# A decoder of two layers on one core: the latent mask added by VectorE, contexts in one run, two stage borders and the experts' order rearranged

## What is computed

```python
# latent attention: queries from the 64 latents (the layer's x), keys and values
# from 64 context tokens and the 64 latents
kv = concat([layer_norm(ctx, g1, b1), ln_lat]) @ Wkv        # 128 tokens per batch
weight = q @ k.T * scale                                   # 16 heads, 64 x 128
weight = where([mask, ones(64)], weight, -max)             # mask only on the 64 context tokens
out = softmax(weight) @ v @ Wout
x = layernorm(x + out)
# experts
gate, idx = max(softmax(x @ router)), argmax(...)
expert e: relu(rows @ w1[e] + b1[e]) @ w2[e] + b2[e]       # its first 512 tokens
x = layernorm(x + gate * expert_output)
```

## Time and profile before

| | |
|---|---|
| three runs | 1677.36, 1677.72, 1684.27 us (median 1677.72) |
| the profiled execution | 1676.6 us, its span 1674.9 us, granted clock 0.989 |
| block 1, block 2, block 3 | to about 390, to about 1044, to the end |
| one pair in the middle of block 3 | 16.20 us |
| busy share of the span | TensorE 96%, weight loads 80%, VectorE 71%, ScalarE 54%, GpSimd 40% |
| DMA | 82.3 MB, 49 GB/s on average |

### The profile page before, as it was taken

The page is one execution under the profiler, slowest core; times in us unless marked ns, Lnnn a source line. Parts: engine busy times, 40 slices in busy tenths (PEclk is TensorE's granted clock), DMA queues, the critical chain, the costliest instruction groups (busy, mean ns, idle before and its releaser), DMA issues. The chain is left out here.

```text
span 1674.9 us, 52009 instructions
## 1 busy us (share of the span) xinstructions
PE 1605.6 (96%) x18188; PEld 1336.8 (80%) x18188; DVE 1183.3 (71%) x3386; ACT 908.5 (54%) x2619; POOL 677.0 (40%) x1070
## 2 busy tenths in 40 slices
PE   7999999998999999999999998899999999999795
PEld 6887788787777777777777776899999999999563
DVE  6889888676777776767777775467777777777654
ACT  5777777643455444544554444565655655656241
POOL 3666666312333333333333332234434444344345
PEclk9999999999999999999999999999999999999998
DMA  3214221121220001110000010121221212212331
GB/s 103 66 47 121 69 56 55 43 64 45 51 53 26 25 27 30 29 28 25 25 25 25 25 31 23 37 60 48 56 60 43 61 41 61 55 47 59 92 98 30
DMA packets 157654, 82.30 MB, mean 49 GB/s; under 512 B 17641, under 2 KB 153115, under 8 KB 157568
## 3 DMA queue, kind: packets, MB, share of 16 engines
q1 hardware_dynamic: 154800, 77.68, 17.4%
q0 software_dynamic: 2048, 3.15, 0.6%
q10 hardware_dynamic: 720, 0.33, 0.1%
HBM read 61.03 MB, written 21.27 MB: 49 GB/s over the span
## 5 line engine op out<-in xcount | busy, mean ns | idle before, releaser
L1477 PE MATMUL bank<-diff_xT,diff_w_score 128*128 128x128 f32 x2048 | 257.0, 279 | 0.7 <-ACT diff_xT L1594 0.7
L1477 PEld LDWEIGHTS bank<-diff_xT,diff_w_score 128*128 128x128 f32 x2048 | 239.3, 192 | 22.6 <-issue 20.2
L1601 ACT ACTIVATE diff_keys<-bank 128x512 f32<-128x512 f32 x256 | 152.4, 595 | 162.2 <-PE bank L1477 162.2
L2273 POOL TENSOR_TENSOR lat_prob<-lat_prob,lat_inv_sum 128x512 f32<-128x512 f32 x128 | 133.4, 1042 | 208.7 <-DVE lat_inv_sum L2198 207.8
L1792 POOL TENSOR_TENSOR diff_prob<-diff_prob,diff_inv_sum 128x512 f32<-128x512 f32 x64 | 67.1, 1049 | 369.6 <-DVE diff_inv_sum L1694 369.6
L2073 ACT ACTIVATE lat_prob<-bank,lat_neg_max 128x128 f32<-128x128 f32 x512 | 180.5, 372 | 1.0 <-DVE lat_neg_max L2218 1.0
L2084 ACT ACTIVATE lat_query<-bank 128x512 f32<-128x512 f32 x128 | 76.5, 597 | 174.3 <-PE bank L1967 159.2
L1997 PE MATMUL bank<-lat_catT,lat_query 128*128 128x128 f32 x1024 | 142.4, 282 | 3.9 <-ACT lat_query L2084 3.9
L1967 PE MATMUL bank<-lat_catT,lat_w_score 128*128 128x128 f32 x1024 | 139.5, 280 | 2.2 <-ACT lat_catT L2065 1.0
L1997 PEld LDWEIGHTS bank<-lat_catT,lat_query 128*128 128x128 f32 x1024 | 125.2, 193 | 15.8 <-issue 10.6
L1977 PE MATMUL bank<-lat_probT,lat_c_rep 32*128 32x256 f32 x2048 | 128.3, 387 | 3.1 <-DVE lat_z L2203 3.1
(11 more groups left out here) (274 smaller groups left out, 3674.4 us busy)
## 6 DMA issues: line engine op xcount, KB each, us to landing
lat_c_rep<-cat SPq DMA_DIRECT2D x128, 128.0 KB
stage<-low_y SPq DMA_DIRECT2D x64, 64.0 KB, 1.6
diff_x_rep<-stage SPq DMA_DIRECT2D x128, 32.0 KB, 1.7
lat_c_t<-cat SPq DMA_DIRECT2D x32, 128.0 KB, 2.2
exp_w<-in_L_ffn_w_dram SPq DMA_DIRECT2D x16, 256.0 KB
expert_rows<-latw_zeros SPq DMA_DIRECT2D x4, 548.0 KB, 5.4
exp_rows<-expert_rows SPq DMA_DIRECT2D x8, 274.0 KB
low_x_t<-in_x_dram SPq DMA_DIRECT2D x32, 64.0 KB, 1.9
```

The lines of the kernel that those rows point to most:

```text
L1477: last = nc.tensor.matmul(ring[(k + d) % 2][:, j * P:(j + 1) * P], w_score[:, H1 * (k // 2) + HS * d + 4 * (k % 2) + j, :], xT[:, :], star ...
L1601: nc.scalar.activation(keys[:, k // 2, 4 * (k % 2):4 * (k % 2) + 4, :].rearrange("p h t -> p (h t)"), ring[(k + d) % 2][:, :], ACT.Copy).t ...
L2273: nc.gpsimd.tensor_tensor(prob[:, q, :, :], prob[:, q, :, :], inv_sum[:, q, :, None].to_broadcast([P, 4, T]), ALU.mult)\
```

## The change

- **Mask.** The identity matmul L2000 goes. VectorE adds the mask in place in PSUM (128 x 256 elements, bf16 mask) before it takes the maximum, and waits on its own semaphore `masked` between the two.
- **Contexts.** Both halves of `contexts(i-1)` stand in c=3, one behind the other. `outputs(i-2)` is cut into 5, 6 and 5 matmuls for c = 0, 1, 2. `z`, its statistics and the variance move from c=1 to c=2 on VectorE, the power from c=2 to c=3 on GpSimd.
- **First border.** TensorE's last feed-forward products stand ahead of the barrier, with five matmuls without use behind them; ScalarE takes the last of the scaled weight copies from VectorE.
- **Second border.** VectorE's three copies of `w_vo` and SyncE's last store of `lat` stand behind the barrier, in block 3; twelve matmuls without use instead of eight. TensorE waits for the `w_vo` copies before the first scores, not before the stage.
- **Last scatter of rows.** GpSimd leaves out `dump` and prepares the token's number before it waits for the destination.
- **Experts.** Three banks for the output products; the rows of e+1 are transposed before the hidden products of e; the hidden products of 7 come before the outputs of 6.
- **Semaphores** of block 3 are no longer cleared by a `give_back` of their own.

```diff
@@ FeedForward.tensor, and its block @@
-        if drain:
-            self.drain(pe, slot)
-        else:
-            pe.wait_ge(self.low.qT_ready, NI)
-            self.slots(pe, slot, between)
+        pe.wait_ge(self.low.qT_ready, NI)
+        self.slots(pe, slot, between)
+        self.drain(pe, slot)
...
             ffn.tensor(pe, lambda g: second.tensor(pe, g, low, weights))
+            core.keep_busy(core.bank[5], 5)
@@ DiffWeights.scalar @@
+        if g in self.multiplied and self.multiplied[g] == self.NQ - 1:
+            act.wait_ge(self.prod_done, 2 * self.NQ)
+            dst, src = self.product(self.NQ - 1, 1)
+            self.nc.scalar.activation(dst, src, ACT.Copy, scale=float(HD1) ** -0.5).then_inc(self.prod_copied, 1)
@@ differential attention @@
-                if have(i, 2):
+                if have(i, 2) and more(i - 2):
                     sp.wait_ge(lat_done, i - 1)
                     store_cat(i - 2, S, lat, lat_stored)
...
                             pe.wait_ge(tri_done, 4)
+                            pe.wait_ge(ffn.z_done, ffn.NG)
...
-            ffn.tensor(pe, drain=True)
...
-            core.keep_busy(core.bank[6], 8)
+            core.keep_busy(core.bank[6], 12)
...
-            latent.take_values(dve)
@@ latent attention @@
-            return core.sem(f"lat_{name}", ctx)
+            return core.sem(f"lat_{name}")
...
+            sp.wait_ge(latent.lat_done, NPAIR)
+            for b in range(2):
+                sp.dma_start(cat[2 * NPAIR - 2 + b, S:T, :], latent.lat[b * S:(b + 1) * S, :]).then_inc(latent.lat_stored, 16)
...
-                    nc.tensor.matmul(ps[:, m * T:(m + 1) * T],
+                    last = nc.tensor.matmul(ps[:, m * T:(m + 1) * T],
                                      query[:, c % 2, b, 2 * hp:2 * hp + 2, :].rearrange("p h s -> p (h s)"),
-                                     catT[:, par, b, :], start=(m == 0), stop=False)
-                nc.tensor.matmul(ps[:, :].rearrange("p (b h t) -> p b h t", b=2, h=2)[:, :, :, 0:S], core.identb[:, :],
-                                 mask_bias[:, bass.ds(2 * i, 2), None, :].to_broadcast([P, 2, 2, S]),
-                                 start=False, stop=True).then_inc(s_done, 1)
+                                     catT[:, par, b, :], start=True, stop=True)
+                last.then_inc(s_done, 1)
...
-                        outputs(i - 2, 0)
+                        outputs(i - 2, 0, 5)
...
-                        outputs(i - 2, 1)
+                        outputs(i - 2, 5, 11)
+                    if c == 2 and live(i - 2):
+                        outputs(i - 2, 11, 16)
...
-                    if c == 2 and live(i - 1):
+                    if c == 3 and live(i - 1):
                         pe.wait_ge(rep_loaded, 64 * i)
                         pe.wait_ge(pT_done, 4 * i)
                         wait(pe, z_done, i - 1)
                         contexts(i - 1, 1 - par, 0)
-                    if c == 3 and live(i - 1):
                         contexts(i - 1, 1 - par, 1)
...
                     if live(i):
+                        if isinstance(i, int) and n == 0:
+                            pe.wait_ge(latent.vo_copied, 4)
                         scores(n, i, c, par)
...
+            def add_mask(i, q):
+                tokens = ps_s[q][:, :].rearrange("p (b h t) -> p b h t", b=2, h=2)[:, :, :, 0:S]
+                nc.vector.tensor_tensor(tokens, tokens, mask_bias[:, bass.ds(2 * i, 2), None, :].to_broadcast([P, 2, 2, S]),
+                                        ALU.add).then_inc(masked, 1)
...
-                    if c == 1 and live(i - 2):
+                    if c == 2 and live(i - 2):
                         dve.wait_ge(res_loaded, 16 * (i - 1))
                         dve.wait_ge(o_done, i - 1)
...
                         dve.wait_ge(s_done, n + 1)
+                        add_mask(i, q)
+                        dve.wait_ge(masked, n + 1)
...
-                    if c == 1 and live(i - 2):
+                    if c == 2 and live(i - 2):
                         nc.vector.bn_aggr(mean_var[:, :], stats[:, :]).then_inc(mv_done, 1)
...
+            dve.wait_ge(latent.mask_done, 3)
+            latent.take_values(dve)
             pairs(dve, pair)
...
-                    if c == 2 and live(i - 2):
+                    if c == 3 and live(i - 2):
                         pool.wait_ge(veps_done, i - 1)
@@ Experts @@
-        self.ps_x, self.ps_out = core.bank[0], [core.bank[1], core.bank[6]]
+        self.ps_x, self.ps_out = core.bank[0], [core.bank[1], core.bank[6], core.bank[7]]
...
-                wait(pe, self.z_done, NR * e + r - 1)
+                wait(pe, self.z_done, NR * e + r - 2)
...
         transpose_rows(0)
-        for e in range(E - 1):
+        for e in range(E):
+            if e + 1 < E:
+                transpose_rows(e + 1)
             hidden(e)
-            transpose_rows(e + 1)
             if e > 0:
                 outputs(e - 1)
-        outputs(E - 2)
-        hidden(E - 1)
         outputs(E - 1)
```

More of the change, by code:

```diff
@@ L850, in sync, with tensor @@
             self.slots(sp, slot, between)
-    def tensor(self, pe, between=None, drain=False):
+    def tensor(self, pe, between=None):
         core, nc, GP, NT = self.core, self.nc, self.GP, FF // P
@@ L1154, in vector @@
             q = self.multiplied[g]
-            for par in range(2):
+            for par in range(1 if q == self.NQ - 1 else 2):
                 dve.wait_ge(self.prod_done, 2 * q + par + 1)
-                src = self.banks[par][:, :].rearrange("p (t d) -> p t d", t=4)
-                dst = self.inputs.w_score[:, :, :].rearrange("p (t o) d -> p t o d", o=2)[:, 4 * q:4 * q + 4, par, :]
+                dst, src = self.product(q, par)
                 self.nc.vector.tensor_scalar(dst, src, float(HD1) ** -0.5, None, ALU.mult).then_inc(self.prod_copied, 1)
@@ L1980, in contexts, with outputs @@
                     last.then_inc(c_done, 1)
-            def outputs(i, odd):
-                for m in range(8):
+            def outputs(i, first, end):
+                for n in range(first, end):
+                    odd, m = n // 8, n % 8
                     last = nc.tensor.matmul(ps_o, ctxT[:, 2 * m + odd, :, :].rearrange("p b s -> p (b s)"),
-                                            w_vo[:, odd, m, :], start=(odd == 0 and m == 0), stop=(odd == 1 and m == 7))
-                if odd:
+                                            w_vo[:, odd, m, :], start=(n == 0), stop=(n == 15))
+                if end == 16:
                     last.then_inc(o_done, 1)
@@ L2250, in scatter @@
             def scatter(i, par):
+                final = isinstance(i, int) and i == NPAIR + 2
                 pool.wait_ge(rows_ready, i - 2)
-                pool.wait_ge(dest_done, i - 2)
-                nc.gpsimd.tensor_tensor(dump[:, :], dump[:, :], dump_step[:, :], ALU.add).then_inc(dump_done, 1)
+                if not final:
+                    pool.wait_ge(dest_done, i - 2)
+                    nc.gpsimd.tensor_tensor(dump[:, :], dump[:, :], dump_step[:, :], ALU.add).then_inc(dump_done, 1)
                 if isinstance(i, int):
@@ L2258, in scatter @@
                 pool.wait_ge(token_done, 2 * (i - 3) + 1)
[L2259 removed]
+                if final:
+                    pool.wait_ge(dest_done, i - 2)
+                else:
+                    nc.gpsimd.tensor_tensor(token[:, :], token[:, :], dump_step[:, :], ALU.subtract).then_inc(token_done, 1)
                 pool.indirect_dma_start(out=xe, out_offset=bass.IndirectOffsetOnAxis(ap=dest[:, 1 - par:2 - par], axis=0),
```

21 lines of the change are left out of this document (11 added, 10 removed).

## The result

The changed kernel took a median of 1660.9 us (1658.2 to 1668.7, 6 runs), the kernel before 1682.2 in the same session (1677.4 to 1684.3): ratio 0.989, interval 0.9868 to 0.9912. The forecast was 1656, its range 1644 to 1671. The profiled execution took 1658.21 against 1676.6, the span 1656.5 against 1674.9: 18.4 us less, where the working had 21.8. Repeated on another chip the ratio was 0.9926 (0.9901 to 0.9951). So the change makes the kernel faster on both: by the ratios 18 us on the first chip and 12 on the other, by the medians 21 and 15.

A forecast was written before the change was run, and what follows sets the result against it. TensorE was taken to pace block 3, then VectorE's chain to z. 13.5 + 0.9 - 1.0 + 4.4 + 2.5 + 0.7 + 0.8 = 21.8 us off 1676.6 gives 1654.8, plus 1.1 for the median: 1656 us, range 1644 to 1671.

The forecast's parts named there:

- The add, 0.45: VectorE in block 3: each mask add and the wait behind it take 0.45 us together.
- Which wait ends last, z: Ahead of the contexts in block 3: TensorE waits last for z, some 0.3 us in each pair.
- The loop, 15.78, rounded to 15.75: VectorE and TensorE, from one eviction of contexts to the next: 15.75 us per pair instead of 16.20, gaining 13.5 us.
- the second one: VectorE's way from the transposition to the reciprocal of c=0, with one add in it: 3.8 us.
- TensorE's floor, 15.40: Rival in block 3: VectorE has unseen slack, TensorE's own list sets 15.40 us per pair, 1645 us in all; chance 0.18.
- First two pairs, 0.9: Start of the latent stage: other waits there, eight masks less on TensorE give 0.9 us.
- Drain, -1.6 to the last eviction: End of the latent stage: one add (0.45) and choose_expert (1.12) ahead of z delay the last contexts, 1.6 us lost.
- Final scatter, +0.6: GpSimd at the latent stage's end: most of 0.7 us of small work ahead of the last scatter goes, gaining 0.6.
- Experts, 4.4: Expert stage: new order and third bank remove TensorE's waits; gain between 1 and 7 us, middle taken, 4.4.
- First border, 2.5: Barrier ahead of the keys: output products moved ahead of it let the keys start sooner, gain 2.5 us (1.5 to 3.5).
- Second border, 0.7: Barrier ahead of block 3: fillers cost 0.5 us but may keep the 2.4 GHz clock; gain 0.7 (-0.6 to 2).
- Semaphores, 0.8: End of the kernel: one clear and barrier less behind the last scatter, gain 0.8 us (0 to 1.4).

The follow-up runs named there:

- z ahead: Changed kernel with z and its statistics moved ahead of the reciprocal of c=2 and choose_expert moved to c=2 on VectorE: 1645.4 us, ratio 0.9836.

## Why the prediction was right, and where it was not

- *The add, 0.45:* this was right. It is 0.43 long, the next instruction starts 0.47 behind its start, and doubled it cost 0.49 in the loop. The estimate made from the Trainium skill (VectorE: DVE Perf Modes, section "The DRAIN you can't avoid") was 0.58; the trace after, like the earlier trace rows, shows no such gap.
- *Which wait ends last, z:* this was right, with 0.44 us per pair instead of some 0.3.
- *The loop, 15.78, rounded to 15.75:* it takes 15.93. The step that was short is the second one, from the transposition to the reciprocal of the next chunk: 3.93 instead of 3.8, because the add of c=0 starts 0.13 later than the maximum did before (1.20 behind the transposition instead of 1.07). The first step was 0.05 short, the third 0.04 long, and 0.03 I rounded away. Together this is 5.4 us over 30 pairs, the largest error of the sum (13.5 against 8.0).
- *TensorE's floor, 15.40:* the number was right (15.41 without mask, 15.42 with z ahead). It was my rival; the kernel as changed doesn't reach it, a reordering of two steps on VectorE does.
- *First two pairs, 0.9:* the first eight pairs gave 3.8, of which 2.1 is the steady gain, so the start gave 1.7.
- *Drain, -1.6 to the last eviction:* the profiles have -2.6. 1.7 of it (5.42 - 3.73) is the clock of the last contexts, which fell in the repeated kernel before as well; 0.9 is left for z, which is late by an add and choose_expert. I had both at their full length.
- *Final scatter, +0.6:* it gave 0.2. From the end of the cast (1568.89) to the scatter there are still 0.76 us, with no other instruction on GpSimd in between, where it was 0.87 before. So most of the 0.7 that I wanted to save is not the small work.
- *Experts, 4.4:* they gave 3.6 in the first session and 1.2 to 1.7 on the later chip. The bounds 1 and 7 held, and the middle of them was a guess. The lower bound is the better description on the later chip: GpSimd's scatters follow each other at the end. The 3.6 have a reason that the prediction doesn't know, z that comes late and a third bank that absorbs it.
- *First border, 2.5:* the number came out at 2.6, for another reason. I took 3.49 at half clock as work that moves ahead of the barrier. Run ahead of it, the products make TensorE arrive later; run behind it at full clock, they cost 0.4 us more than that. The rest of the 2.6 belongs to the clock (1.8) and to a start 0.4 sooner.
- *Second border, 0.7:* the profiles have 1.5, of which 1.0 is the clock behind the border and 0.5 that of the first keys (from them to the next keys 6.80 before, 6.23 after). At equal clock it is about -0.2.
- *Semaphores, 0.8:* 0.6 from the end of the last scatter to the end of the span.
- *Ahead of the border, 2.7:* this is in no term. There is a stretch of half clock in the low attention's end (granted 0.91 from 305 to 325 in the profile of before, 1.00 after), in code that the change does not touch. Profiles of the changed kernel and its variants with 0.91 there reach the mark at 385.4 to 386.7 instead of 387.2, so up to 1.8 of the 2.7 us has another reason, which stays open.

So the forecast lay inside its own range for the right chain, with one step mis-sized. How close the sum came is partly luck: the terms at the first and second border were right only by the clock. If the stretches ahead of the border (2.7), at the first border (1.8), at the first keys (0.5) and behind the second border (1.0) are taken off and the drain's 1.7 put back, 14 of the 18.4 us are left. That is an estimate. With the smaller gain in the experts it comes near the 12 us that the ratio gives for the second chip (its medians give 15).

## What to carry to other kernels

When two cuts shorten the same engine's list and both pay with the same second engine, cost them together: here each alone was worth 0.4 us a pair and both 0.27. An instruction that another engine waits for belongs ahead of the wait that its own engine makes anyway. Removing work in front of such a wait gave nothing (0.01 us a pair), because the wait grew by it; only with the awaited instruction moved ahead of the wait as well did it give 0.5 us a pair. Compare stretches of equal granted clock before any microsecond at a border is credited to an edit, and look at a second execution of the kernel before as well: its drain ran at full clock once and at half clock once.

## What the runs showed of the hardware

- The granted clock after a border or a drain differs between executions of one kernel. The last contexts of the kernel before took 3.73 us in one and 5.42 in another, behind equal waits of 3.10 and 3.11 us. The time of a run follows the clock: the changed kernel took 1658.6 to 1659.1 at a mean of 0.990, 1664.4 at 0.985 and 1670.6 at 0.981, all on one chip.
- The same code of the experts ran differently in different sessions: z followed z after about 0.9 us on the two chips of the middle sessions, and often after about 1.5 in the first and the last session, while TensorE's loads kept their pace (31 in 3.54 us). The old order took 7.44 us per expert on the one and about 8.0 on the other, the new order 7.44 on both.
- An in-place add on PSUM with a broadcast bf16 operand, 256 elements per partition, takes 0.43 us, as a read of PSUM of that size does.
